# Computing a diagonal chunk of a symmetric product from its diagonal on, and transposing the rest

## The reference

```
v     = groupnorm(x)                            # (4, 256, 4096)
g     = g_w v + g_b                             # 256 -> 128 channels
f     = einsum('bcn,bcm->bnm', v, v)            # (4096 x 4096) an image, symmetric
attn  = softmax(f, axis=-1)
y     = einsum('bnm,bcm->bcn', attn, g)
wy    = batchnorm(W_w y + W_b) * gamma + beta   # over images and points
out   = x + wy + v
```

## Time and profile before

| what | value |
|---|---|
| median of 3 runs | 2401.73 us |
| profiled execution, its time | 2396.38 us |
| its span, first to last instruction | 2394.6 us |
| PE busy / DVE / ACT / POOL | 91% / 71% / 45% / 37% |
| mean granted PE clock | 0.975 of 2.4 GHz |

### The profile page before, as it was taken

One profiled execution on the slowest core, in us unless ns is written; L12 is line 12 of the kernel. 1 busy time (PEld: TensorE's weight loads), 2 busy tenths in 40 slices (PEclk: granted clock), 3 DMA queues, 4 the chain that ended last, 5 costly groups with the idle time before them and its releaser, 6 DMA issues.

```text
span 2394.6 us, 32898 instructions
## 1 busy us (share of the span) xinstructions
PE 2170.7 (91%) x9520; PEld 1526.9 (64%) x9520; DVE 1690.0 (71%) x3062; ACT 1085.4 (45%) x2206; POOL 892.7 (37%) x624
## 2 busy tenths in 40 slices
PE   6899999997899999989889899998799999999878
PEld 4787766654587776655568677665458777665323
DVE  5565667878755666789766666787975576676876
ACT  3334445453444444445343444445434444444435
POOL 3001233568401013459531112346850102345860
PEclk9999999999999999999999999999999999999989
DMA  3121234544312223544412223353441232345869
GB/s 133 75 99 69 93 102 131 189 116 154 128 53 77 107 84 111 166 147 137 164 56 94 74 89 107 119 185 115 156 152 41 84 110 87 108 140 190 279 216 352
DMA packets 108412, 304.59 MB, mean 127 GB/s; under 512 B 11456, under 2 KB 11968, under 8 KB 93888
## 3 DMA queue, kind: packets, MB, share of 16 engines
q1 hardware_dynamic: 108224, 302.37, 37.4%
HBM read 159.71 MB, written 142.61 MB: 126 GB/s over the span
## 4 chain that ended last, share of the span: by engine, by line
PE 60%; POOL 15%; issue 13%; DVE 6%; ACT 3%; DMA 2%; DVEq 0%; SPq 0%; POOLq 0%; ACTq 0%
PE bank L1102 9%; PE bank L1104 8%; PE bank L1103 8%; PE bank L1157 8%; PE bank L1137 7%; POOL fy_d L674 5%; POOL fy_c L674 5%; PE bank L1161 4%; PE bank L1163 4%; PE bank L1162 4%; PE bank L1293 2%; ACT ring L740 2%; DVE lacc L956 2%; POOL xl L647 2%; PE bank L1223 2%
## 5 line engine op out<-in xcount | busy, mean ns | idle before, releaser
L766 ACT CAST phi<-bank 128x512 fp32r<-128x512 f32 x480 | 280.8, 587 | 905.1 <-PE bank L1137 904.9
L1102 PE MATMUL bank<-xh 128*128 128x512 f32 x1152 | 538.1, 467 | 38.8 <-DVE colmax L911 26.8
L903 DVE TENSOR_SCALAR_CACHE_REDUCE ring<-bank 128x512 f32<-128x512 f32 x576 | 395.1, 686 | 235.3 <-PE bank L1104 184.3
L1104 PE MATMUL bank<-xh,xl 128*128 128x512 f32 x1152 | 459.1, 399 | 0.0
L1103 PE MATMUL bank<-xl,xh 128*128 128x512 f32 x1152 | 456.1, 396 | 0.0
L1137 PEld LDWEIGHTS bank<-ident,ring 128*128 128x128 f32 x1920 | 237.5, 144 | 239.8 <-issue 141.0
L938 DVE TENSOR_TENSOR plo<-bank,phi 128x512 fp32r<-128x512 f32 x480 | 325.7, 683 | 90.8 <-ACT phi L766 56.2
L1137 PE MATMUL bank<-ident,ring 128*128 128x128 f32 x1920 | 301.7, 281 | 91.4 <-DVE plo L938 50.4
L674 POOL TENSOR_TENSOR fy_c<-fy_c,maxrow 128x512 f32<-128x512 f32 x200 | 294.1, 1472 | 188.5 <-DMA fy_c<-spill 188.3
L674 POOL TENSOR_TENSOR fy_d<-fy_d,maxrow 128x512 f32<-128x512 f32 x188 | 277.6, 1479 | 212.8 <-DMA fy_d<-spill 212.8
L740 ACT ACTIVATE ring<-ring,nmax 128x512 f32<-128x512 f32 x480 | 344.5, 719 | 0.0
(11 more groups left out here) (109 smaller groups left out, 2770.4 us busy)
## 6 DMA issues: line engine op xcount, KB each, us to landing
spill<-ring SPq DMA_DIRECT2D x112, 1024.0 KB, 4.4
fy_c<-spill SPq DMA_DIRECT2D x200, 256.0 KB, 4.0
fy_d<-spill SPq DMA_DIRECT2D x188, 256.0 KB, 3.7
ring<-x_dram SPq DMA_DIRECT2D x40, 512.0 KB, 4.8
lbuf<-spill SPq DMA_DIRECT2D x60, 256.0 KB, 4.1
yd<-yn SPq DMA_DIRECT2D x32, 256.0 KB, 3.2
fx_a<-x_dram SPq DMA_DIRECT2D x16, 512.0 KB, 7.2
out_dram<-fx_a SPq DMA_DIRECT2D x16, 512.0 KB, 4.5
```

Of the source, the lines that this page charges most:

```text
L903: last = nc.vector.tensor_scalar(ring[:, SLOT[u], t, :], src, 1.0, None, ALU.mult, ALU.max, accum_out=rowm[:, t, c:c + 1])
L1102: nc.tensor.matmul(dst, xh[:, k, rows], xh[:, k, cols], start=(k == 0), stop=False)
L1104: last = nc.tensor.matmul(dst, xl[:, k, rows], xh[:, k, cols], start=False, stop=(k == K - 1))
```

## The change

Only `multiply` on PE changes. For a diagonal chunk, row tile t is computed from column t x 128 of the block on: 512, 384, 256 and 128 columns for t = 0 to 3. The t squares of 128 x 128 left of that are filled by transposing the squares above the diagonal that DVE has copied into `ring` with the products before; they are written into the same PSUM bank. As the last of these squares is in product t - 1, PE waits between the matmuls and the transposes until DVE has taken product s - 1. DVE's work, and that of ACT, POOL and SP, is the same instructions in the same order.

```diff
@@ -1096,12 +1096,19 @@
                 if s >= 2 or not first:
                     pe.wait_ge(f_taken, n * NPROD + s - 1)
                 rows = slice(j * W + t * P, j * W + (t + 1) * P)
-                cols = slice(c * W, (c + 1) * W)
-                dst = fps[:, s % 2, :]
+                own = t * P if c == j else 0
+                cols = slice(c * W + own, (c + 1) * W)
+                dst = fps[:, s % 2, own:]
                 for k in range(K):
                     nc.tensor.matmul(dst, xh[:, k, rows], xh[:, k, cols], start=(k == 0), stop=False)
                     nc.tensor.matmul(dst, xh[:, k, rows], xl[:, k, cols], start=False, stop=False)
                     last = nc.tensor.matmul(dst, xl[:, k, rows], xh[:, k, cols], start=False, stop=(k == K - 1))
+                if own:
+
+                    pe.wait_ge(f_taken, n * NPROD + s)
+                    for above in range(t):
+                        last = nc.tensor.transpose(fps[:, s % 2, above * P:(above + 1) * P],
+                                                   ring[:, SLOT[CHUNK_NO[j, c]], above, own:own + P], ident[:, :])
                 last.then_inc(f_made, 1)
```

## The result

The changed kernel takes 2358.92 us, the median of 4 runs (2354.97 to 2365.9), against 2401.34 us of the kernel before beside it (4 runs, 2396.69 to 2404.8): ratio 0.9834, 95% interval 0.9804 to 0.9865. In a second group of five rounds it was 2361.97 against 2403.16, ratio 0.9849 (0.9816 to 0.9882). By the ratios that is 40 and 36 us gained, by the medians 42 and 41, where 14.4 were forecast.

A forecast was written before the change was run, and what follows sets the result against it. PE was taken to set most of the time, not all. Terms 20 + 2 - 4.8 - 1.8 + 1 - 2 = 14.4 us gained, from 2396.4 to 2382.0, median forecast 2387 us; range 2374 to 2404.

The forecast's parts named there:

- PE sets the time in stages 0 to 4: PE time saved in stages 0 to 4 should shorten the program, by about 5.5 us an image.
- The pitches: Matmuls with 384, 256 and 128 columns take 0.171, 0.114 and 0.110 us; each added transpose takes 0.11.
- The straight line: Alternative pitches between the two known points: 0.189 us for 384 columns, 0.149 for 256; net 0.75 us a chunk.
- 20 us for the chunks (1,1) to (5,5): In these 20 chunks the new wait is over before it is reached, so each gains 1.0 us.
- 2 us for (6,6): Chunk (6,6) gains 0.5 us in each of four images; its fourth product's saving is not seen.
- -6.6 us for the seven chunks of stage 5: New waits exceed savings: chunk (7,7) loses 1.2 us in four images, (0,0) loses 0.6 in images 1 to 3.
- 0.3 more on each chunk (7,7): PE leaves chunk (7,7) 0.9 us later; put at 1.2 because the first wait also delays DVE before its second take.
- -2 us for the clock: Whole program: new waits and short matmuls leave PE less occupied, costing 2 us, with ends of +4 and -8.
- the first chunk of image 0: Chunk (0,0) of image 0, at the start with DVE idle, gains 1 us.
- The waits cost nothing: Rival, chance 0.19: late PE is absorbed in stages 5 and 6; gain 24 us, time 2377 us.
- The gain is swallowed: Rival, chance 0.17: DRAM transfers and POOL set when left tiles are ready; gain 0 to 4 us, 2398 to 2402.
- The clock falls: Rival, chance 0.12: clock stays low longer after pauses at stage starts; with 60 us more, 2415 us.

The follow-up runs named there:

- cut: The kernel before with five full matmuls left out of each chunk (1,1) to (6,6), no transposes or new waits: 2363.7 us, ratio 0.9845.
- no_wait: The changed kernel without the new wait, its transposes reading the identity matrix instead: 2356.0 us, ratio 0.9828 to the kernel before.
- cost_alone: The kernel before with all matmuls at full width, plus the new wait and six transposes a chunk: 2409.9 us, ratio 1.0041.

## Why the prediction was wrong

- *PE sets the time in stages 0 to 4.* Right: cut and the change gain the same, and 5.5 us an image shorter was 6.2 in image 1.
- *The pitches.* Right: 0.171, 0.114, 0.110 assumed, 0.176, 0.119, 0.112 measured, which with 0.228 for 512 columns saves 1.66 us a chunk for 1.73. The straight line (0.189, 0.149) was wrong. The transposes at 0.11: right within the error, 21.4 ± 1.5 us for 21.1. The Trainium skill ("TensorE: Matmul & The Clock Gate", section "Back-to-back issue gap") gives an isolated gap of 56 ns for 128 columns. This type in this stream has 112 ns.
- *20 us for the chunks (1,1) to (5,5).* Somewhat low: 24.3 ± 2.1 by the runs, 21.6 by the stages of image 3.
- *2 us for (6,6), because DVE never stands still behind it.* Wrong: 4.4 ± 1.5 by the runs, 7.6 by the stages of image 3. DVE not standing still does not mean that its work is fixed: its addition went from 1.48 to 0.69 us when it came ahead of POOL's subtraction.
- *-6.6 us for the seven chunks of stage 5.* Wrong: the net is -0.9 ± 1.5. That PE's lateness goes on to the end was not the error: of 10 us of waits, 7.3 ± 2.6 came off when no_wait took them out, against the 7 saved. The waits themselves were too long in the sum. Those of (7,7) in images 0 to 2 were forecast to 0.1 us each (0.4 and 1.3 for 0.5 and 1.4), but image 3 has 1.3 in place of 1.9, and (0,0) 1.3 in place of 1.8: 10 us for 13.0. On top of that I had put 0.3 more on each chunk (7,7), which nothing bears out. Whether DVE also absorbs some of the waits, the runs are too coarse to say.
- *-2 us for the clock.* This is the step that failed by most: +13 us, with the sign the other way. I reasoned that new waits and short matmuls leave PE less occupied, and gave the good side an end of +4. The runs show a mean clock of 0.9792 for 0.9722, and cut, without waits or short matmuls, has 0.9777; so the step from less occupied to a lower clock is what failed. What raises the clock is not known. The mean clock over many runs, not the one in one profile, was the number to have: 0.9722 for the kernel before, of which its profile (0.975) was a good run. Of the 26 us by which 14.4 falls short of 40, the clock is 15, stage 5 is 6, and the chunks (1,1) to (6,6) are 7, less 1 to 2 for the first chunk of image 0, whose gain of 1 is lost in the error.
- *The rivals.* "The waits cost nothing" gave 24 us and was nearest, yet not for its reason: the waits cost 7. "The gain is swallowed" was wrong: 24.3 us came from the chunks (1,1) to (5,5). "The clock falls" named the right quantity and the wrong way. The Trainium skill ("TensorE: Matmul & The Clock Gate", section "Part 4: PE-mode transpose") says that transposes don't count for the clock in the way matmuls do, which spoke for that rival. cost_alone, which only adds 192 transposes and the waits, was at 0.9782, above the kernel before, so no run here bears out a lower clock from them; it doesn't isolate the statement either.

## What to carry to other kernels

Where PE sets the pace, columns saved and transposes added can be summed at their pitches from the trace, and the sum holds to a few us (20 for 21.6 or 24.3 here), as long as no other engine's work changes its length with the moment at which it starts. Before a change of one or two per cent is forecast or judged, look at the mean granted clock of many runs of the kernel before: here 0.001 of it is 1.9 us, as much as two chunks, and one profile does not give it. A new wait is read from the trace before, but in every place where it comes, not in one image; here 10 us of waits cost 7.3 ± 2.6. Putting it behind the next piece of work that doesn't need it took most of the idle time away and may be worth 3 us, which the timing alone can't tell from nothing.

## What was not expected of the hardware

- A 128 x 512 addition on DVE took 0.69 us when it began just ahead of a subtraction of POOL and 1.48 us when POOL had begun one 0.33 us before; the subtraction then takes 1.27 us, and 1.74 when DVE came first.
- In one group of runs, the same program had a mean granted clock from 0.965 to 0.979 and times from 2413 to 2386 us; the same pause of 1.83 us is followed by a stretch at 1.2 GHz in one image and not in another.
- A kernel with 21 us more work (cost_alone) was only 8 us slower as timed, ratio 1.0041 (1.0017 to 1.0064), since its clock was higher by 0.006. A longer span with the same time at the lower clock would give less than 0.001 (an estimate: 133 us at half speed in 2401 or in 2422). That stays unexplained.
